# A graph network's scatter: masks and equal-key counts fused into one VectorE instruction, and one-hots of destinations made once per group of 8 chunks

## What is computed

```
# layer 1: normalised graph convolution (L0)
out = segment_sum(dinv[row] * w * dinv[col] * (x @ kernel)[col], row)    ; relu(out + bias)
# layer 2: messages along each edge in both directions (L1)
msg_fwd  = [H[heads], E] @ W_fwd  + b_fwd      # E: 206250 x 128 edge attributes
msg_back = [H[tails], E] @ W_back + b_back
agg = segment_sum([msg_fwd, msg_back], [tails, heads]) / count
x   = layernorm(leaky(agg) + H) * gamma + beta
```

## Time and profile before

| | us |
|---|---|
| three runs | 4732.38, 4742.2, 4747.09; median 4742.2 |
| profiled execution | 4736.39, its span 4734.6 |
| busy in the span | PE 3462.1 (73%), DVE 3722.4 (79%), POOL 2819.5 (60%), ACT 1851.2 (39%) |

### The profile page before, as it was taken

How to read it: one execution, slowest core, us unless ns; L and a number is a source line. 1 busy time by engine, 2 the same in 40 slices (tenths; PEclk the granted TensorE clock), 3 DMA queues, 4 the chain that set the end, 5 groups by cost and what they waited for, 6 DMA issues and landing times. The chain is left out here.

```text
span 4734.6 us, 104535 instructions
## 1 busy us (share of the span) xinstructions
PE 3462.1 (73%) x30910; PEld 2929.9 (62%) x31114; DVE 3722.4 (79%) x11962; ACT 1851.2 (39%) x4574; POOL 2819.5 (60%) x1705
## 2 busy tenths in 40 slices
PE   3555317888887888778888523798888888998955
PEld 3445217777776767677777422677777777776645
DVE  8999729998889888898899445887878777864527
ACT  1011004544444444444444313444444444455513
POOL 0000168888888888888888603787777777860000
PEclk8777659998989999999899766899999999999977
DMA  9990118888878777887788785455555555557031
GB/s 170 315 104 0 43 37 144 144 139 141 142 136 143 139 137 139 141 142 140 134 141 141 124 142 122 72 83 80 81 77 81 81 82 79 82 78 84 4 89 28
DMA packets 679953, 518.82 MB, mean 110 GB/s; under 512 B 305948, under 2 KB 592548, under 8 KB 677736
## 3 DMA queue, kind: packets, MB, share of 16 engines
q0 software_dynamic: 256640, 183.99, 34.6%
q1 hardware_dynamic: 422724, 327.85, 28.7%
HBM read 288.51 MB, written 249.53 MB: 114 GB/s over the span
## 5 line engine op out<-in xcount | busy, mean ns | idle before, releaser
L705 POOL DMA_INDIRECT gcn_sums<-fl_sums,fl_to_i x1008 | 1655.0, 1642 | 362.5 <-issue 160.2
L1531 POOL DMA_INDIRECT gcn_sums<-shared,ds_to_i x608 | 1038.0, 1707 | 486.6 <-ACT shared L1781 306.8
L929 ACT COPY fl_sums<-bank 128x256 f32<-128x256 f32 x1008 | 378.0, 376 | 662.2 <-PE bank L857 571.2
L1736 PE MATMUL bank<-ds_counts,ds_parts 128*128 128x256 bf16 x3675 | 595.5, 275 | 0.0
L852 PE MATMUL bank<-fl_sum_hot,fl_attrs 128*128 128x128 f32 x2016 | 404.9, 307 | 169.5 <-DVE attr_sums L721 169.4
L1805 ACT COPY ds_turned<-bank 128x1024 bf16<-128x1024 bf16 (+1 forms) x325 | 313.1, 963 | 537.7 <-PE bank L1721 534.7
L852 PEld LDWEIGHTS bank<-fl_sum_hot,fl_attrs 128*128 128x128 f32 x2016 | 328.3, 210 | 300.0 <-issue 259.9
L1769 ACT CAST ds_counts<-bank 128x392 bf16<-128x392 f32 x800 | 379.1, 491 | 234.9 <-PE bank L1679 222.0
L371 PE MATMUL bank<-places,row_hot 128*128 128x200 bf16 x1616 | 267.6, 292 | 255.4 <-DVE places L324 255.4
L856 PE MATMUL bank<-fl_pay,fl_same 128*128 128x128 f32 x2016 | 420.5, 292 | 30.2 <-DVE fl_same L741 23.1
L742 DVE SCALAR_TENSOR_TENSOR fl_earlier<-fl_key_b,fl_pat,before_me 128x128 bf16<-128x128 bf16 x1008 | 442.0, 439 | 0.0
(11 more groups left out here) (238 smaller groups left out, 8098.5 us busy)
## 6 DMA issues: line engine op xcount, KB each, us to landing
fl_attrs<-in_edge_attr SPq DMA_DIRECT2D x126, 512.0 KB, 4.6
shared<-in_edge_attr SPq DMA_DIRECT2D x150, 256.0 KB
fl_rel_b<-dst_offset SPq DMA_DIRECT2D x126, 256.0 KB
fl_key_b<-src_key SPq DMA_DIRECT2D x126, 256.0 KB
gcn_sums<-zeros SPq DMA_DIRECT2D x40, 640.0 KB
shared<-src_key SPq DMA_DIRECT2D x76, 256.0 KB, 4.0
gcn_sums<-fl_sums,fl_to_i POOLq DMA_INDIRECT x1008
near<-src_float SPq DMA_DIRECT2D x1, 12892.0 KB
```

What stands on the lines that cost most here:

```text
L705: nc.gpsimd.indirect_dma_start(out=d.tab_gcn[j % K], out_offset=bass.IndirectOffsetOnAxis(ap=to_i[:, (GPI * kk + gi) % 4, j:j + 1], axis=0 ...
L929: nc.scalar.copy(sums[:, h, j, :], sum_bank[j % 2][:, 0:2 * F]).then_inc(staged, 1)
L1531: nc.gpsimd.indirect_dma_start(out=d.tab_gcn[j % K].rearrange("n (two f) -> (n two) f", two=2), out_offset=bass.IndirectOffsetOnAxis(ap=to ...
L1736: ins = nc.tensor.matmul(row_bank[:, 0:2 * P], parts[:, tile, s, :], counts[:, h, tile, :, :].rearrange("p b q -> p (b q)"), start=(tile = ...
```

## The change

`same` is now made by the two-input instruction that used to make `earlier`. Its mask is `from_me` (q not below p) in place of `before_me`, its output is `same` in float32, and its accumulator counts the equal keys from p on, p among them (`later`). The last edge of a key, no longer the first, now keeps the real row, and the test is `later > 1.5`. The separate `same` instruction goes. `spread_hot` of a whole group becomes one instruction at j = 2. `sum_hot` of a whole group becomes one two-input instruction (`spot_sums`), which is not made ahead any more: it stands at j = 0 of its own group, before `add_window` of the group before, once TensorE has finished that group. One small instruction of the `to_i` chain goes in the first layer. SyncE issues the records after offsets and keys, and behind one more wait.

```diff
+            nc.vector.tensor_tensor(d.from_me[:], d.iota[:], d.part[:, 0:1].to_broadcast([P, P]), ALU.is_ge)
...
                     sp.sem_inc(load_turns, 1)
-                    sp.dma_start(flat(rec[:, h, :, :]), d.rec[bass.ds(g, 1), :, :].rearrange("o p r -> (o p) r")).then_inc(rec_in[h], 16)
                     sp.dma_start(flat(rel_b[:, h, :, :]), everywhere(d.dst_offset, g)).then_inc(rel_in[h], 16)
                     sp.dma_start(flat(key_b[:, h, :, :]), everywhere(d.src_key, g)).then_inc(key_in[h], 16)
+                    at_least(sp, sum_ready, g - 1)
+                    sp.sem_inc(load_turns, 1)
+                    sp.dma_start(flat(rec[:, h, :, :]), d.rec[bass.ds(g, 1), :, :].rearrange("o p r -> (o p) r")).then_inc(rec_in[h], 16)
...
+            def spot_sums(g, h):
+
+                at_least(dve, summed, J * g)
+                nc.vector.tensor_tensor(sum_hot[:], d.iota[:].unsqueeze(1).to_broadcast([P, J, P]), rec[:, h, 2, :].unsqueeze(2).to_broadcast([P, J, P]),
+                                        ALU.is_equal).then_inc(sum_ready, 1)
...
-                if ahead and j % U == 0:
-                    dve.wait_ge(row_ready, 2 * (g - 1) + j // U + 1)
-                nc.vector.tensor_scalar(spread_hot[:, j, :], rel_b[:, h, :, j], d.part[:, 0:1], None, ALU.is_equal).then_inc(spread_ready, 1)
...
-                nc.vector.tensor_scalar(same[:, j, :], key_p[:, h, :, j], pat_f[:, j:j + 1], None, ALU.is_equal).then_inc(same_ready, 1)
-                counted = nc.vector.scalar_tensor_tensor(earlier[:, j, :], key_p[:, h, :, j], pat_f[:, j:j + 1], d.before_me[:],
-                                                         ALU.is_equal, ALU.mult, accum_out=before[:, j:j + 1])
+                nc.vector.scalar_tensor_tensor(same[:, j, :], key_p[:, h, :, j], pat_f[:, j:j + 1], d.from_me[:],
+                                               ALU.is_equal, ALU.mult, accum_out=later[:, j:j + 1]).then_inc(same_ready, 1)
+                if j == 2:
+                    dve.wait_ge(rel_in[h], 16 * loads(i, kk, gi))
+                    at_least(dve, row_ready, 2 * g)
+                    nc.vector.tensor_scalar(spread_hot[:], rel_b[:, h, :, :].rearrange("p q j -> p j q"), d.part[:, 0:1], None,
+                                            ALU.is_equal).then_inc(spread_ready, 1)
                 if j == J - 1:
-                    counted.then_inc(step, 1)
-                for jj in (range(4) if j == 3 else range(j, j + 1) if j > 3 else ()):
-                    nc.vector.tensor_scalar(sum_hot[:, jj, :], d.iota[:], rec[:, h, 2, jj:jj + 1], None, ALU.is_equal).then_inc(sum_ready, 1)
...
-                    nc.vector.scalar_tensor_tensor(to_f[:], before[:], 0.0, to_f[:], ALU.is_gt, ALU.mult).then_inc(step, 1)
+                    nc.vector.scalar_tensor_tensor(to_f[:], later[:], 1.5, to_f[:], ALU.is_gt, ALU.mult).then_inc(step, 1)
...
-                    nc.vector.tensor_copy(to_i[:, (GPI * kk + gi) % 4, :], to_f[:]).then_inc(to_ready, 1)
+                    nc.vector.tensor_tensor(to_i[:, (GPI * kk + gi) % 4, :], to_f[:], rec[:, h, 0, :], ALU.add).then_inc(to_ready, 1)
...
                     gi, j = divmod(c, J)
+                    if j == 0:
+                        spot_sums(group(i, kk, gi), gi % 2)
                     if j == 0 and not (first and gi == 0):
                         add_window(group(i, kk, gi) - 1)
...
-                pe.wait_ge(spread_ready, J * g + U * (half + 1))
+                pe.wait_ge(spread_ready, g + 1)
...
-                if j >= 2:
-                    pe.wait_ge(sum_ready, ch + 1)
+                    pe.wait_ge(sum_ready, g + 1)
```

More of the change, by code:

```diff
@@ L605, in first_layer @@
         sum_hot = sb("sum_hot", [P, J, P])
-        earlier = sb("earlier", [P, J, P], BF16)
-        before = sb("before", [P, J])
+        later = sb("later", [P, J])
         pat = sb("pat", [P, J], I32)
@@ new lines, in prepare @@
+                if j == 2:
[3 more added lines that the diff above has]
+                                            ALU.is_equal).then_inc(spread_ready, 1)
+                if j == J - 1:
+                    dve.wait_ge(same_ready, J * (g + 1))
+                    nc.vector.scalar_tensor_tensor(to_f[:], later[:], 1.5, to_f[:], ALU.is_gt, ALU.mult).then_inc(step, 1)
+                    dve.wait_ge(step, 2 * g + 2)
@@ L1570, in cut_chunk, with spot_sums @@
                 nc.vector.memset(src_sums[:, c * CHUNK * F:(c + 1) * CHUNK * F], 0.0).then_inc(src_zeroed, 1)
+            def spot_sums(q, p):
+                at_least(dve, chunk_done, J * q)
+                nc.vector.tensor_tensor(sum_hot, d.iota[:].unsqueeze(1).to_broadcast([P, J, P]), rec[:, p, 2, :].unsqueeze(2).to_broadcast([P, J, P]),
+                                        ALU.is_equal).then_inc(sum_ready, 1)
             def add_window(q):
@@ L1587, in prepare @@
                     dve.wait_ge(key_in[p], 16 * loads(i, h, gi))
[L1588 removed]
+                    dve.wait_ge(step, 3 * q + 1)
                 if ahead:
                     dve.wait_ge(chunk_done, J * (q - 1) + j + 1)
[L1591 to L1593 removed]
+                nc.vector.scalar_tensor_tensor(same[:, j, :], key_p[:, p, :, j], pat_f[:, j:j + 1], d.from_me[:],
+                                               ALU.is_equal, ALU.mult, accum_out=later[:, j:j + 1]).then_inc(same_ready, 1)
                 if j == J - 1:
[L1595 to L1601 removed]
+                    dve.wait_ge(same_ready, J * (q + 1))
+                    nc.vector.scalar_tensor_tensor(to_f[:], later[:], 1.5, to_f[:], ALU.is_gt, ALU.mult).then_inc(step, 1)
+                    dve.wait_ge(step, 3 * q + 2)
                     nc.vector.tensor_tensor(to_f[:], to_f[:], rec[:, p, 0, :], ALU.add).then_inc(step, 1)
[L1603 removed]
+                    dve.wait_ge(step, 3 * q + 3)
                     for k in range(K):
@@ L1611, in beside_step @@
                 gi, j = divmod(c, J)
+                if j == 0:
+                    spot_sums(behind(i, h, gi), gi % 2)
                 if j == 0 and gi > -PG:
@@ L2133, in program @@
         d.before_me = sb("before_me", [P, P])
+        d.from_me = sb("from_me", [P, P])
         d.spare = sb("spare", [P, J])
```

28 lines of the change are left out of this document (5 added, 23 removed).

## The result

The changed kernel takes 4801.0 us (median of 4 runs, 4787.3 to 4801.7), the kernel before 4742.5 us beside it. The ratio is 1.0119, its 95% interval 1.0095 to 1.0144. I had forecast 4715 us.

What follows compares the result with a forecast made beforehand. POOL's scatters were taken to bound the first layer, VectorE the dense opening, TensorE the tiles. First layer -14, opening -9 and tiles -4 gave -27 us, from 4742 to 4715; own range 4690 to 4745, full range 4665 to 4800.

Steps and rivals of the forecast that it cites:

- Net +21, of which two thirds: +14 us: First-layer scatters: VectorE's changed operations delay POOL by a net 21 us by formula, of which two thirds, +14 us, counted.
- d²/2T: First-layer delay of POOL by a VectorE operation lasting d, scatter period T 1.98 us; summed to 124 us, measured 83.
- credit of 39 us: First layer: the part of the formula's 124 us of scatter delay that the change was to remove.
- None of that is on POOL's path: First layer: VectorE's saved work gains only from 35 us of late scatter starts, of which 25 were counted.
- I cost this at 0: First layer: TensorE's wait for `sum_hot` and then the window addition was taken as hidden, 0 us.
- The bound without cover, 145: First layer: TensorE time lost to the later window addition if nothing hides it, 126 x 1.15 = 145 us.
- `spread_hot` at 0.8 us: First layer: time of the single 1024-element instruction, priced like a row of 3200; bounds 1.3 and at worst 1.9 us.
- Tiles -4 us: Dense stage, 18 tiles: TensorE's two waits a tile for the window addition change by net -0.25 us a tile.
- the start 3 us earlier: First layer's start: shorter preparation of the first group lets the first scatter begin about 3 us sooner (0 to 4.6).
- The opening: Dense stage's opening, bounded by VectorE: 4 groups prepared there each lose 2.4 us, -9 us (0 to -12).
- C: Rival, chance 0.20: in the first layer long operations meet POOL's start in every group; excess 177 us, kernel 4795 us.
- D: Rival, chance 0.10: TensorE's window wait takes over, `sum_hot` exposed in each group; tiles +41 us, kernel 4785 us.

Runs made afterwards that it cites:

- e1: The changed kernel, but `sum_hot` reads the numbers 0 to 127 from PSUM instead of SBUF in both stages; 4771.6 us.
- e7: The changed kernel, but `sum_hot` is made by two instructions of 4 chunks, a group ahead, in both stages; 4755.4 us.
- e6: The kernel before, with only the fused mask and count added in both stages; `sum_hot` and `spread_hot` stay small instructions; 4681.1 us.
- e12: e6 with one unread small VectorE instruction per chunk put back in the first layer; 4714.0 us.
- e11: e6 plus, in the first layer, the long `sum_hot` with its numbers in PSUM, the short `to_i` chain and later record loads; 4715.7 us.
- e5: The kernel before, with only the fused mask and count added, in the dense stage alone; 4706.4 us.
- e10: e6 with `spread_hot` as one instruction of 1024 elements at step 2 in the first layer; 4720.9 us.
- e8: The changed kernel's first layer with a second, unread `sum_hot` instruction ahead of the real one, and the old dense stage; 4819.1 us.
- e2: The changed kernel, but `sum_hot` is made by eight one-input instructions at its new place, in both stages; 4810.3 us.

## Why the prediction was wrong

The prices on record add up to the result: mask -37, `spread_hot` +31, lock of `sum_hot` +36, its late place +27 make +57 for the first layer, measured +49. They fit e1 as well (2041 - 36 = 2005, measured 2008), but not e7: the mask, `spread_hot` and half of the lock make +12 there, 2004 us, and it took 2042. So the account is shown for the changed kernel, and how the parts act on each other is open.

On the profiled executions the forecast missed by 91 us (-27 against +64): 44 in the scatters (+14 forecast, +58 measured), 16 in POOL's gaps (-25, -9), 24 in the tiles (-4, +20), 6 in the opening (-9, -3), 1 in the rest. Against the prediction's steps:

- **"Net +21, of which two thirds: +14 us" is the step that failed first.** The sum d²/2T was scaled by 83/124 for all operations alike. For `sum_hot` the unscaled 42 us were right to the tenth (42.0 by the count), and for `spread_hot` 18 had been put in against 13.2 measured. The short ones are overrated by the formula, and `fl_hi_w`, three back to back, is underrated (28 us, measured 37.8). The credit of 39 us for the removed ones was too large as well: the small one-input instructions had caused 11.3 us of excess before (5.5 + 4.0 + 1.8). In all the scatters grew by 58 us instead of 14.
- **"None of that is on POOL's path, so as work it is worth nothing beyond the 35 us of late starts."** Wrong: the mask's 242 us gave 37 (e6), and they come back when the work does (e12). I took 76 waits of ScalarE for a sign that the queue before POOL was full; beside them stood 613 waits for TensorE, which I did not weigh. Near its pace POOL still paid for late work, and in e6 the excess fell with the gaps: 23 and 13 us.
- **"I cost this at 0, covered by TensorE's idle fifth and the queue before POOL."** The later place costs 27 us (e11 against e6; record loads and `to_i` chain in it). The bound without cover, 145, was far too high.
- **`spread_hot` at 0.8 us.** It takes 1.11 to 1.40 us; the row of 3200 contiguous elements was not its like, the bound 1.3 was nearer. It was booked as a saving and costs 31 us.
- **Tiles -4 us; measured +20.** The waits were sized well (46.0 us; I had 50.1 - 4). The mask took one of the two waits of a tile away (e5), and `sum_hot` made the other one longer, 2.38 to 2.63 us. What I missed is that the clock drops beside it: 78 us at the lower level instead of 27. e5 and e7 show tiles with the mask and without so long a wait. By the means above the mask alone gives the tiles 20 us, and the long `sum_hot` takes 41.
- **What held:** `sum_hot` at 1.22 us, the start 3 us earlier, VectorE's busy time down by over 400 us, POOL's 0.30 us gaps. The opening gave 3 of its 9 us.

Of the rivals, C came nearest in number (4795) and in its mark (mean scatter above 1.69; it is 1.700), though only 77 scatters start in the 126 instructions. Its number is in part luck: it put the excess at 177 us, measured 141, and the later place and the tiles, which it gave no cost, made up for the rest. D's mark was half right: tiles of 69 us, but the wait not above 70. The range ended at 4800 and missed by 1 us. Its upper end came from C alone, while `spread_hot`, the later place and the tiles all went the same way beside it.

## What to carry to other kernels

Take the parts of a fused change one by one: here the mask gained 56 us, and the rest lost some 115. In a stage whose pace is POOL's indirect DMA, price a VectorE instruction by its length squared and by its operands, not by its busy time, and give it one PSUM input if it must be long. Where TensorE is the bound, look at the longest single wait and not at the sum, and keep batched work off the place just before the instruction that releases it.

## What the runs showed of the hardware

- A scatter that starts in a 1.22 us VectorE operation with two SBUF inputs takes up to 2.60 us instead of 1.56; with one of the inputs in PSUM it takes 1.56 to 1.60 (77 scatters of e11). VectorE's own time is the same (median 1224 ns both ways).
- A one-input operation of 1024 strided bf16 elements (1.15 us) delays a scatter as well: on average 0.34 us (e10) to 0.73 us (e8) for those that start in it, over seven runs. An addition with an input in PSUM (`gcn_t`) doesn't by itself: 0.1 us in 61 scatters before. In e1 102 scatters that start in one carry 6.9 us, nearly all in ten after which a masked count follows within 0.6 us of the scatter's start.
- POOL mostly gets its turn between two long operations issued back to back: in e8 in 69 of 69 cases, and the excess grew by 38 us, where one lock of 2.3 us would have brought 126 by the formula. Not always: before, 9 of 54 delayed scatters that start in `ds_lo_hot` wait for the `ds_hi_hot` behind it too, the one of the earlier trace rows among them.
- TensorE's granted clock halved for 3.4 to 6.8 us at 14 of 18 waits of 2.38 to 2.63 us, and at none of 18 waits of 1.22 to 1.34 us (e7). e2, with still longer waits (up to 3.1 us), had 106 us of it. No run changed such a wait alone, so the length of the wait is the likeliest cause, not a shown one.
